# Softmax sums inside the value product, and the division between two 32x32-block turns on VectorE

## The chip, the cores and the metric

One Trainium2 chip, of which the kernel uses one core. The metric is the device time of one execution in microseconds: median of three runs 378.38 (377.3 to 379.06). The profile is of one further execution, whose span from the first to the last instruction is 376.4 us.

## The reference

128 sequences of 64 tokens with 128 features (`x`), and a context of the same shape. Two blocks follow each other.

The first is cross attention with 16 heads of 8 features: queries from the normalised `x`, keys and values from the context.

```
qh, kh, vh = split_heads(q @ W_q + b_q), split_heads(k @ W_k + b_k), split_heads(v @ W_v + b_v)
probs = softmax(einsum('bhqd,bhkd->bhqk', qh, kh) / sqrt(8))
out   = merge_heads(einsum('bhqk,bhkd->bhqd', probs, vh)) @ W_o + b_o
x     = x + tanh(g_xattn) * out
```

The second is a feed-forward network with 8 experts: a small gate picks one expert per token, and the token goes through that expert's two layers (128 to 256 to 128, exact gelu), times its gate probability and tanh(g_ffn), added to `x`.

## The kernel before

All of it is one program with an order written out by hand for each engine. 8192 tokens are 64 tiles of 128 tokens (two sequences of 64); four tiles are a chunk (512 tokens, 16 chunks).

**First stage.** A loop over 76 slots (`SLOTS`, lines 242, 449, 587, 967 and 1242: every engine has the same loop, GpSimd by chunks). In slot k several tiles are under way at once, each with a fixed lag: scores for the row maxima of tile k-4 (`scores1`, L1121), their maxima on VectorE (L976, two halves), final scores of tile k-10 in fp32 (`scores2`, L1104 and L1111), their exponentials on ScalarE in two halves (L596, L598), the value product of tile k-11 and the output projection of tile k-12 (`values`, L1166 to L1198). Once per chunk come the transposes of xn and of the context (L1263, L1216), the projections of keys (L1223), queries (L1281) and values (L1288), and of the maxima (L1271), which ScalarE copies as mS (L645) and GpSimd turns into a mask product MD (L443) that the scores of that chunk need.

The exponentials lie as PT: on the partitions the 64 keys of one head and, below them, the 64 keys of its neighbour; on the columns 16 blocks (8 head pairs of 2 sequences) of 64 queries. For two heads at a time the value product multiplies 32 columns of V (8 of one head that meet only the upper 64 partitions, 8 of the other that meet only the lower 64, 16 zeros) with 64 columns of PT. The result in PSUM (`pv`, columns 0 to 127) holds head and feature on the partitions and tokens on the columns: two such products are added into each group of 32 partitions, the second shifted by 16. The sums of the exponentials come from a second set of matmuls: `kz` holds ones where V holds values, so that `pv` columns 128 to 255 hold each sum eight times, on the partitions where its head's values lie (L1184, eight matmuls of 128 columns). VectorE takes 128x128 reciprocals of them (L982, `rec`), adds the projection of the tile before to the residual (L988, `XR`, with the semaphore x1_ok), and multiplies values and reciprocals (L993, `OT`, ot_ok). TensorE multiplies OT by W_o in the next slot (L1195). In fp32 each matmul is two instructions in the trace.

`values` waits, before its first matmul, for x1_ok and ot_ok of the slot before. Its one signal to VectorE, pv_ps, comes with its last matmul.

In each slot VectorE goes through: maxima (L976), reciprocal, XR, OT, then `stat_sum` (L716) and `stat` (L708) for a later tile's layer norm, and in some slots a part of the routing (peak, lead, pick, count, place, gate: six slots of every twelve, two to four small instructions each). `route_place` waits for GpSimd's g_pay.

GpSimd has in each chunk: the mask product (L443), the layer norm's powers and its four products (L352 to L360, L375), the residual with the bias (L367), the second norm's power (L384, L386), and from chunk 8 on four record sends (L400, an indirect DMA of one tile's rows each into the expert-sorted buffer `records`), later eight.

**Second stage.** 71 tiles of sorted tokens: load (SP), normalise (VectorE), transpose and two layers (TensorE, L1228, L1236, L1323, L1326), gelu (ScalarE), combine (VectorE, L1037), and a scattered store per tile from GpSimd (L471).

Of the kernel before, what the change touches and what calls it, by code (L numbers as in the profile page):

```python
# [13 lines left out]
P = 128  # L14
D = 128
H = 16
# [46 lines left out]
def gated_block(nc, x, ctx_in, g_xattn, g_ffn, W_q, b_q, W_k, b_k, W_v, b_v, W_o, b_o, w_red, wg, W1, b1, W2, b2, out):  # L63
    es = ExitStack()
    with es:
# [6 lines left out]
        def sem(name):  # L72
            return es.enter_context(nc.semaphore(name))
# [20 lines left out]
        kz = sb("kz", [P, 48])  # L94
# [44 lines left out]
        rec = sb("rec", [P, P])  # L139
# [36 lines left out]
        kz_ok, perm_ok, brow_ok, bvb_ok, sel_ok = (sem(n) for n in ("kz_ok", "perm_ok", "brow_ok", "bvb_ok", "sel_ok"))  # L176
# [15 lines left out]
        pv_ps, rec_ok, ot_ok, x1_ok = (sem(n) for n in ("pv_ps", "rec_ok", "ot_ok", "x1_ok"))  # L192
# [485 lines left out]
        def _(dve):  # L678
# [8 lines left out]
            link(nc.vector.memset(kz[:, :], 0.0))  # L687
            nc.vector.memset(kz[0:S, 16:16 + DK], 1.0)
            nc.vector.memset(kz[S:P, 16 + DK:32], 1.0).then_inc(kz_ok, 1)
# [68 lines left out]
            def make_masks():  # L758

                with nc.allow_low_precision("zeros and ones"):  # L760
                    nc.vector.tensor_reduce(imask[:, :], ident[:, :].rearrange("p (a i l) -> p i a l", i=2, l=2),
                                            mybir.AxisListType.XY, ALU.add).then_inc(imask_ok, 1)
                link(nc.vector.tensor_reduce(usum[:, :].rearrange("p (a o) -> p a o", o=1),
                                             ident[:, :].rearrange("p (t a i) -> p a t i", t=RT, i=HI),
                                             mybir.AxisListType.XY, ALU.add))
                dve.wait_ge(par_ok, 1)
                link(nc.vector.tensor_tensor(upar[:, :, :], usum[:, 0:CU].rearrange("p (u o) -> p u o", o=1).to_broadcast([P, CU, 2]),
                                             par[:, :].rearrange("p (o l) -> p o l", o=1).to_broadcast([P, CU, 2]), ALU.mult))
                nc.vector.tensor_copy(usel[:, :, :, :].rearrange("p u l k -> p (u l) k"),
                                      upar[:, :, :].rearrange("p u (l o) -> p (u l) o", o=1).to_broadcast([P, 2 * CU, S])  # L770
                                      ).then_inc(sel_ok, 1)

# [194 lines left out]
            for k in range(SLOTS):  # L967
# [12 lines left out]
                if 0 <= n < NU:  # L980
                    dve.wait_ge(pv_ps, pv_turn(k))
                    nc.vector.reciprocal(rec[:, :], pv[:, P:2 * P]).then_inc(rec_ok, 1)  # L982
# [8 lines left out]
                if 0 <= n < NU:  # L991
                    dve.wait_ge(rec_ok, n + 1)
                    nc.vector.tensor_tensor(OT[n % 2][:, :], pv[:, 0:P], rec[:, :], ALU.mult).then_inc(ot_ok, 1)  # L993
                if j == 1 and 2 <= s < NC + 2:
                    x_logits(s - 2)
                if 2 * CU <= k + 6 < NU:
                    stat_sum(k + 6)
                if 2 * CU <= k + 7 < NU:
                    stat(k + 7)
# [9 lines left out]
                if k == 10:  # L1009
                    split_biases()  # L1010
                if k in gate_done_at:
                    route_gate(gate_done_at[k])
# [48 lines left out]
        def _(pe):  # L1061
# [104 lines left out]
            def values(k):  # L1166
                n, no = k - LAGV, k - LAGO
                if k == LAGV:
                    pe.wait_ge(kz_ok, 1)
                    pe.wait_ge(wox_ok, 1)  # L1170
                if no >= 1:
                    pe.wait_ge(x1_ok, min(no, NU))
                if no >= 0:
                    pe.wait_ge(ot_ok, min(no + 1, NU))
                last = None
                if 0 <= n < NU:
                    c, u = n // CU, n % CU
                    pe.wait_ge(pt_ok, n + 1)
                    if u == 0:
                        pe.wait_ge(v_ok, c + 1)  # L1180
                    vf = V[c % 3][:, :, :, :].rearrange("p u h r -> p (u h r)")
                    for i in range(2):
                        for t in range(RT):
                            nc.tensor.matmul(pv[32 * t:32 * t + 32, P:2 * P].rearrange("p (b q) -> p b q", b=2),  # L1184
                                             kz[:, 16 - 16 * i:48 - 16 * i], PT[n % 2][:, HI * t + i:HI * t + HI:2, :],
                                             start=(i == 0), stop=False, skip_group_check=True)
                    for i in range(2):
                        for b in range(2):
                            for t in range(RT):
                                at = 32 * (H * u + 8 * b + 2 * t + i) - 16 * i  # L1190
                                last = nc.tensor.matmul(pv[32 * t:32 * t + 32, S * b:S * b + S], vf[:, at:at + 32],  # L1191
                                                        PT[n % 2][:, HI * t + 2 * b + i, :], start=False, stop=(i == 1),
                                                        skip_group_check=True)
                if 0 <= no < NU:
                    last = nc.tensor.matmul(pv[:, 2 * P:2 * P + DX], OT[no % 2][:, :], wox[:, :], start=True, stop=True,  # L1195
                                            skip_group_check=True)
# [173 lines left out]
```

## Time and profile before

| | |
|---|---|
| runs, us | 378.38, 377.3, 379.06 |
| span of the profiled execution | 376.4 us (the page gives no other time of it) |
| TensorE busy | 332.6 us (88%) |
| VectorE busy | 290.0 us (77%) |
| GpSimd busy | 266.9 us (71%) |
| ScalarE busy | 242.3 us (64%) |
| mean granted TensorE clock | 0.963 of full speed |

Full speed of TensorE is 2.4 GHz; a granted clock of 0.5 is 1.2 GHz. Busy time is the union of an engine's instructions; consecutive instructions overlap at their ends, so what an instruction costs its engine is read from start to start in a timeline. "Idle before" with a releaser says which engine's semaphore ended a wait; "issue" is time in which the profile shows nothing waited for.

### The profile page before, as it was taken

The numbers are of one execution on the slowest core, as the hardware profiler recorded it, in microseconds if no ns is written. First come the engines' busy times: TensorE is split into PE (matmuls) and PEld (weight loads), VectorE is DVE, ScalarE is ACT, GpSimd is POOL, SyncE is SP. The second block draws the span as 40 slices with busy tenths as digits, with TensorE's granted clock in tenths as the row PEclk, the third lists the DMA queues.
The fourth block names the chain that finished last, engine by engine and source line by source line (L and its number), as shares of the span: only waits on it lengthen the run. The fifth ranks groups of instructions, "written<-read, shape, count | busy, mean of one in ns | idle before, by whom it ended". The sixth has DMA issues, their size and how long they took to land.

```text
span 376.4 us, 17275 instructions
## 1 busy us (share of the span) xinstructions
PE 332.6 (88%) x6654; PEld 261.4 (69%) x6654; DVE 290.0 (77%) x900; ACT 242.3 (64%) x604; POOL 266.9 (71%) x349
## 2 busy tenths in 40 slices
PE   3878999999999999999999997776888999999960
PEld 1534776776776777876876866655776899999950
DVE  7777788889899898989899799966578666666630
ACT  3747688788788788788788885644443455555520
POOL 6494664474685898798796876787557777777771
PEclk9978999999999999999999999997699999999995
DMA  5344334323313423323211121143014433333210
GB/s 114 105 141 141 102 95 129 111 80 98 118 48 98 139 80 105 95 70 102 71 63 51 44 93 50 41 129 97 36 56 132 137 120 99 114 110 100 66 46 0
DMA packets 47164, 34.13 MB, mean 91 GB/s; under 512 B 9800, under 2 KB 42955, under 8 KB 47083
## 3 DMA queue, kind: packets, MB, share of 16 engines
q1 hardware_dynamic: 42440, 23.90, 22.6%
q0 software_dynamic: 4352, 9.00, 6.6%
q8 instruction: 54, 0.88, 1.0%
q14 instruction: 26, 0.21, 0.2%
q10 hardware_dynamic: 292, 0.13, 0.1%
HBM read 17.13 MB, written 10.04 MB: 72 GB/s over the span
## 4 chain that ended last, share of the span: by engine, by line
PE 62%; issue 9%; POOL 9%; DVE 8%; ACT 6%; SPq 2%; DMA 1%; POOLq 0%; DVEq 0%; ACTq 0%
PE m L1326 10%; PE sc L1236 8%; PE pv L1184 7%; POOL records L400 6%; PE pv L1191 5%; PE sc L1111 5%; PE pv L1195 5%; PE m L1288 4%; PE sc L1121 3%; PE sc L1104 3%; PE sc L1228 2%; PE m L1323 2%; ACT PT L598 1%; PE m L1263 1%; PE m L1216 1%
## 5 line engine op out<-in xcount | busy, mean ns | idle before, releaser
L976 DVE TENSOR_REDUCE mx<-sc 128x8 f32<-128x512 f32 x128 | 82.2, 684 | 20.7 <-PE sc L1121 20.2
L471 POOL DMA_INDIRECT out<-fo,rr x71 | 70.0, 986 | 23.3 <-issue 19.3
L400 POOL DMA_INDIRECT records<-XR,pos x64 | 63.4, 991 | 20.4 <-issue 16.4
L982 DVE RECIPROCAL rec<-pv 128x128 f32<-128x128 f32 x64 | 61.1, 954 | 10.4 <-PE pv L1195 5.2
L596 ACT ACTIVATE PT<-sc 128x512 f32<-128x512 f32 x64 | 38.1, 595 | 28.2 <-issue 20.1
L1326 PE MATMUL m<-w,fgT 128*128 x284 | 50.7, 302 | 0.1
L1236 PE MATMUL sc<-fxT,w1s 128*128 128x128 f32 x284 | 45.6, 284 | 4.2 <-DVE w1s L964 3.3
L1037 DVE SCALAR_TENSOR_TENSOR fo<-m,rr 128x128 f32<-128x128 f32 x71 | 24.9, 350 | 29.8 <-PE m L1326 29.8
L1184 PE MATMUL pv<-PT,kz 128*32 128x128 f32 x1024 | 41.7, 281 | 6.5 <-DVE XR L988 5.9
L375 POOL TENSOR_SCALAR xn<-XC,mv,rstd 128x128 f32<-128x128 f32 x56 | 44.2, 799 | 0.0
L1236 PEld LDWEIGHTS sc<-fxT,w1s 128*128 128x128 f32 x284 | 38.6, 197 | 6.5 <-ACT fxT L578 4.2
L578 ACT ACTIVATE fxT<-sc 128x128 f32<-128x128 f32 x71 | 19.7, 278 | 35.4 <-PE sc L1228 35.4
L1191 PE MATMUL pv<-PT,V 128*32 128x64 f32 x2048 | 41.3, 220 | 0.2 <-issue 0.2
L1326 PEld LDWEIGHTS m<-w,fgT 128*128 128x128 f32 x284 | 38.0, 194 | 2.6 <-issue 0.4
L1111 PE MATMUL sc<-Qd,kT 32*128 32x128 f32 x1024 | 39.8, 270 | 0.0
L584 ACT ACTIVATE fgT<-sc 128x256 f32<-128x256 f32 x71 | 27.3, 384 | 18.7 <-PE sc L1236 18.3
L598 ACT ACTIVATE PT<-sc 128x512 f32<-128x512 f32 x64 | 38.3, 598 | 0.0
L1191 PEld LDWEIGHTS pv<-PT,V 128*32 128x32 f32 x2048 | 37.6, 111 | 0.3 <-issue 0.3
L1184 PEld LDWEIGHTS pv<-PT,kz 128*32 128x32 f32 x1024 | 24.5, 109 | 14.5 <-DVE XR L988 7.2
L1111 PEld LDWEIGHTS sc<-Qd,kT 32*128 32x128 f32 x1024 | 34.4, 186 | 0.0
L1195 PE MATMUL pv<-wox,OT 128*128 128x137 f32 x128 | 32.5, 336 | 0.0
L352 POOL TENSOR_TENSOR rstd<-ve,mhalf 128x4 f32<-128x4 f32 x16 | 16.5, 1034 | 21.6 <-DVE ve L721 21.4
(207 smaller groups left out, 681.3 us busy)
## 6 DMA issues: line engine op xcount, KB each, us to landing
rr<-records SPq DMA_DIRECT2D x71, 72.0 KB, 2.0
XC<-in_x SPq DMA_DIRECT2D x16, 256.0 KB, 3.2
C<-in_ctx SPq DMA_DIRECT2D x16, 256.0 KB, 3.1
Qd<-Qf SPq DMA_DIRECT2D x64, 64.0 KB
Kd<-kb SPq DMA_DIRECT2D x64, 32.0 KB
w<-in_L_ffn_W SPq DMA_DIRECT2D x16, 128.0 KB, 2.8
out<-fo,rr POOLq DMA_INDIRECT x71, 2.3
w1l<-in_L_ffn_W SPq DMA_DIRECT2D x8, 128.0 KB, 3.3
```

The source lines that it names most:

```text
L375: i = nc.gpsimd.tensor_scalar(xn[:, u, :], XC[c % 3][:, u, :], mv[c % 2][:, u, 0:1], rstd[:, u:u + 1], ALU.subtract, ALU.mult)
L400: nc.gpsimd.indirect_dma_start(out=records, out_offset=bass.IndirectOffsetOnAxis(ap=pos[:, u:u + 1], axis=0), in_=XR[:, u, :], in_offset=N ...
L471: nc.gpsimd.indirect_dma_start(out=out_rows, out_offset=bass.IndirectOffsetOnAxis(ap=rr[q][:, R_ID:R_ID + 1].bitcast(U32), axis=0), in_=fo ...
L598: nc.scalar.activation(pt[:, 2:4], sc[:, 2:4, 256:512], ACT.Exp).then_inc(pt_ok, 1)
L976: nc.vector.tensor_reduce(mx[c % 2][:, t:t + 2, HI * u:HI * u + HI], sc[:, t:t + 2, 0:256].rearrange("p t (i k) -> p t i k", i=HI), AX_X, ...
L982: nc.vector.reciprocal(rec[:, :], pv[:, P:2 * P]).then_inc(rec_ok, 1)
L1111: m = nc.tensor.matmul(sc[:, t, 256 + P * b:256 + P * b + P].rearrange("p (i q) -> p i q", i=2), kT[c % 3][r, u, b, :, :].rearrange("r l k ...
L1184: nc.tensor.matmul(pv[32 * t:32 * t + 32, P:2 * P].rearrange("p (b q) -> p b q", b=2), kz[:, 16 - 16 * i:48 - 16 * i], PT[n % 2][:, HI * t ...
L1191: last = nc.tensor.matmul(pv[32 * t:32 * t + 32, S * b:S * b + S], vf[:, at:at + 32], PT[n % 2][:, HI * t + 2 * b + i, :], start=False, st ...
L1195: last = nc.tensor.matmul(pv[:, 2 * P:2 * P + DX], OT[no % 2][:, :], wox[:, :], start=True, stop=True, skip_group_check=True)
L1236: i = nc.tensor.matmul(sc[:, 2 + p, P * m:P * m + P], w1s[p][:, P * m:P * m + P], fxT[p][:, :], start=True, stop=True, skip_group_check=True)
L1326: i = nc.tensor.matmul(o, fgT[p][:, m, :], w2[:, bass.ds(e, 1), m, :].rearrange("p o c -> p (o c)"), start=False, stop=(m == HH - 1), skip ...
```

## The change

V gets its sums: two more of the 32 columns that each pair of heads has hold a one on the upper, and on the lower 64 partitions (columns 16 and 17), written once per buffer by `v_sums` from `hsel`. ScalarE rewrites only columns 0 to 15 for each chunk. So each value product also yields the two heads' sums. The products of even and odd pairs are no longer added into one another but go to columns of their own, and fill 256 columns of `pv`.

VectorE turns these 256 columns in blocks of 32x32 into `TV`, which puts tokens on the partitions; there a head's sum is one number per token, and 16 reciprocals per partition do for 128. `NV` is the product of values and reciprocals with the 14 idle columns left out, and a second turn of 128 columns brings OT back into its old form. XR, stat_sum and stat are set between the four steps.

TensorE's value product waits for the first turn (`tv_ok`) and x1_ok; the wait for ot_ok moves to in front of the projection.

```diff
-            link(nc.vector.memset(kz[:, :], 0.0))
-            nc.vector.memset(kz[0:S, 16:16 + DK], 1.0)
-            nc.vector.memset(kz[S:P, 16 + DK:32], 1.0).then_inc(kz_ok, 1)
+            link(nc.vector.memset(hsel[:, :], 0.0))
+            nc.vector.memset(hsel[0:S, 0:1], 1.0)
+            nc.vector.memset(hsel[S:P, 1:2], 1.0).then_inc(hsel_ok, 1)
...
+            def v_sums(i):
+
+                dve.wait_ge(hsel_ok, 1)
+                dve.wait_ge(zero_p, i + 1)
+                nc.vector.tensor_copy(V[i][:, :, :, 2 * DK:2 * DK + 2].rearrange("p u h r -> p (u h) r"),
+                                      hsel[:, :].rearrange("p (o l) -> p o l", o=1).to_broadcast([P, CU * H, 2])
+                                      ).then_inc(vden_ok, 1)
...
-                    nc.vector.reciprocal(rec[:, :], pv[:, P:2 * P]).then_inc(rec_ok, 1)
+                    nc.vector.transpose(TV[:, :, :].rearrange("p a r -> p (a r)"), pv[:, 0:2 * P]).then_inc(tv_ok, 1)
...
+                    dve.wait_ge(tv_ok, n + 1)
+                    nc.vector.reciprocal(rec[:, :, :], TV[:, :, 2 * DK:2 * DK + 2]).then_inc(rec_ok, 1)
+                if 2 * CU <= k + 6 < NU:
+                    stat_sum(k + 6)
+                if 0 <= n < NU:
                     dve.wait_ge(rec_ok, n + 1)
-                    nc.vector.tensor_tensor(OT[n % 2][:, :], pv[:, 0:P], rec[:, :], ALU.mult).then_inc(ot_ok, 1)
+                    nc.vector.tensor_tensor(NV[:, :, :, :], TV[:, :, 0:2 * DK].rearrange("p a (l d) -> p a l d", l=2),
+                                            rec[:, :, :].rearrange("p a (l o) -> p a l o", o=1).to_broadcast([P, 2 * CU, 2, DK]),
+                                            ALU.mult).then_inc(nv_ok, 1)
+                if 2 * CU <= k + 7 < NU:
+                    stat(k + 7)
+                if 0 <= n < NU:
+                    dve.wait_ge(nv_ok, n + 1)
+                    nc.vector.transpose(OT[n % 2][:, :], NV[:, :, :, :].rearrange("p a l d -> p (a l d)")).then_inc(ot_ok, 1)
                 if j == 1 and 2 <= s < NC + 2:
                     x_logits(s - 2)
-                if 2 * CU <= k + 6 < NU:
-                    stat_sum(k + 6)
-                if 2 * CU <= k + 7 < NU:
-                    stat(k + 7)
...
+                if k in (3, 4, 7):
+                    v_sums((3, 4, 7).index(k))
...
                 if k == LAGV:
-                    pe.wait_ge(kz_ok, 1)
+                    pe.wait_ge(vden_ok, 3)
                     pe.wait_ge(wox_ok, 1)
                 if no >= 1:
                     pe.wait_ge(x1_ok, min(no, NU))
-                if no >= 0:
-                    pe.wait_ge(ot_ok, min(no + 1, NU))
...
+                    if n >= 1:
+                        pe.wait_ge(tv_ok, n)
                     vf = V[c % 3][:, :, :, :].rearrange("p u h r -> p (u h r)")
-                    for i in range(2):
-                        for t in range(RT):
-                            nc.tensor.matmul(pv[32 * t:32 * t + 32, P:2 * P].rearrange("p (b q) -> p b q", b=2),
-                                             kz[:, 16 - 16 * i:48 - 16 * i], PT[n % 2][:, HI * t + i:HI * t + HI:2, :],
-                                             start=(i == 0), stop=False, skip_group_check=True)
                     for i in range(2):
                         for b in range(2):
                             for t in range(RT):
-                                at = 32 * (H * u + 8 * b + 2 * t + i) - 16 * i
-                                last = nc.tensor.matmul(pv[32 * t:32 * t + 32, S * b:S * b + S], vf[:, at:at + 32],
-                                                        PT[n % 2][:, HI * t + 2 * b + i, :], start=False, stop=(i == 1),
-                                                        skip_group_check=True)
+                                at = 32 * (H * u + 8 * b + 2 * t + i)
+                                last = nc.tensor.matmul(
+                                    pv[32 * t:32 * t + 32, P * b:P * b + P].rearrange("p (h i q) -> p i h q", h=2, i=2)[:, i],
+                                    vf[:, at:at + 32], PT[n % 2][:, HI * t + 2 * b + i, :].rearrange("p (h q) -> p h q", h=2),
+                                    start=True, stop=True, skip_group_check=True)
                 if 0 <= no < NU:
+                    pe.wait_ge(ot_ok, no + 1)
                     last = nc.tensor.matmul(pv[:, 2 * P:2 * P + DX], OT[no % 2][:, :], wox[:, :], start=True, stop=True,
                                             skip_group_check=True)
```

## Rows read from the trace of the kernel before

**Rows 1.** Table of stretches: length, busy us (instructions) by engine, PEclk, DMA, GB/s.

```profile
core 0: us, PE busy (x) PEld busy (x) DVE busy (x) ACT busy (x) POOL busy (x), PEclk, DMA share, GB/s
38.90:118.90 80.00, 77.99 (x2074) 58.97 (x2071) 68.55 (x184) 64.64 (x149) 46.86 (x88) 1.00 0.35 101
118.90:214.76 95.86, 94.19 (x2516) 71.27 (x2508) 84.57 (x229) 79.42 (x187) 81.72 (x105) 1.00 0.26 82
214.76:256.80 42.04, 33.73 (x1028) 26.48 (x1020) 36.09 (x121) 25.21 (x67) 31.33 (x36) 1.00 0.27 81
256.80:269.30 12.50, 9.03 (x84) 7.64 (x78) 7.60 (x27) 5.18 (x18) 8.06 (x9) 0.61 0.17 54
```

**Rows 2.** Timeline of TensorE in one slot: start, length, line, count.

```profile
171.24 0.29 PE L1104 MATMUL sc<-MD,usel 32*128 32x256 bf16 x4
...
171.91 0.32 PE L1121 MATMUL sc<-Kd,qb 32*64 32x256 bf16 x8
172.16 0.64 PE L1184 MATMUL pv<-PT,kz 128*32 128x128 f32 x16
172.62 0.63 PE L1191 MATMUL pv<-PT,V 128*32 128x64 f32 x32
173.18 0.50 PE L1195 MATMUL pv<-wox,OT 128*128 128x137 f32 x2
...
174.57 0.29 PE L1104 MATMUL sc<-MD,usel 32*128 32x256 bf16 x4
```

**Rows 3.** Timeline of ScalarE: exponentials of one slot and of the next.

```profile
159.35 0.60 ACT L596 ACTIVATE PT<-sc 128x512 f32<-128x512 f32 x1 [1.02 <-issue]
...
159.90 0.60 ACT L598 ACTIVATE PT<-sc 128x512 f32<-128x512 f32 x1
...
162.75 0.60 ACT L596 ACTIVATE PT<-sc 128x512 f32<-128x512 f32 x1
```

**Rows 4.** Groups of instructions by line (whole run, reciprocal of 12 of 120:214).

```profile
L976 DVE TENSOR_REDUCE mx<-sc 128x8 f32<-128x512 f32 x128 | 82.2, 684 | 20.7 <-PE sc L1121 20.2
...
L982 DVE RECIPROCAL rec<-pv 128x128 f32<-128x128 f32 x64 | 61.1, 954 | 10.4 <-PE pv L1195 5.2
...
L993 DVE TENSOR_TENSOR OT<-pv,rec 128x128 f32<-128x128 f32 x64 | 17.9, 280 | 0.0
...
L862 DVE RECIPROCAL col<-col 128x12 f32<-128x12 f32 x2 | 0.5, 228 | 0.1
```

**Rows 5.** Timeline of VectorE in one slot.

```profile
184.29 0.96 DVE L982 RECIPROCAL rec<-pv 128x128 f32<-128x128 f32 x1
185.16 0.26 DVE L988 SCALAR_TENSOR_TENSOR XR<-pv,tg,XR 128x137 f32<-128x137 f32 x1
185.34 0.28 DVE L993 TENSOR_TENSOR OT<-pv,rec 128x128 f32<-128x128 f32 x1
...
186.33 1.29 DVE L976 TENSOR_REDUCE mx<-sc 128x8 f32<-128x512 f32 x2 [0.44 <-PE sc L1121]
```

**Rows 6.** GpSimd: waits (total, times, longest) of 126:257, and its timeline.

```profile
POOL MD L443 <- ACT mS L645: 8.5, 7, 2.1
POOL records L400 <- DVE XR L863: 1.6, 2, 0.8
...
186.07 0.60 POOL L443 TENSOR_TENSOR MD<-mS,imask 128x256 bf16<-128x256 bf16 x1 [1.23 <-ACT mS L645]
...
200.28 0.60 POOL L443 TENSOR_TENSOR MD<-mS,imask 128x256 bf16<-128x256 bf16 x1 [1.27 <-ACT mS L645]
```

**Rows 7.** Timeline: products on VectorE with both inputs in SBUF, and GpSimd beside them.

```profile
149.93 3.15 POOL L375 TENSOR_SCALAR xn<-XC,mv,rstd 128x128 f32<-128x128 f32 x4
...
150.63 0.24 DVE L845 TENSOR_TENSOR ky<-ky,oh 128x96 f32<-128x96 f32 x1
...
228.85 0.61 POOL L443 TENSOR_TENSOR MD<-mS,imask 128x256 bf16<-128x256 bf16 x1 [2.10 <-ACT mS L645]
...
229.13 0.41 DVE L817 TENSOR_TENSOR ex<-ex,col 128x64 f32<-128x64 f32 x1
```

**Rows 8.** GpSimd's stores, by line, 269.3 to 368.7 us.

```profile
L471 POOL DMA_INDIRECT out<-fo,rr x71 | 70.0, 986 | 23.3 <-issue 19.3 <-DVE fo L1037 4.0
```

More of the change, by code:

```diff
@@ L93, in gated_block @@
         clog = sb("clog", [P, NX])
-        kz = sb("kz", [P, 48])
+        hsel = sb("hsel", [P, 2])
         usum = sb("usum", [P, 8])
@@ L138, in gated_block @@
         PT = [sb(f"PT{i}", [P, H, S]) for i in range(2)]
-        rec = sb("rec", [P, P])
+        TV = sb("TV", [P, 2 * CU, 32])
+        rec = sb("rec", [P, 2 * CU, 2])
+        NV = sb("NV", [P, 2 * CU, 2, DK])
         OT = [sb(f"OT{i}", [P, P]) for i in range(2)]
@@ L175, in gated_block @@
         pstep, one_ok = sem("pstep"), sem("one_ok")
-        kz_ok, perm_ok, brow_ok, bvb_ok, sel_ok = (sem(n) for n in ("kz_ok", "perm_ok", "brow_ok", "bvb_ok", "sel_ok"))
+        hsel_ok, vden_ok, perm_ok, brow_ok, bvb_ok, sel_ok = (sem(n) for n in ("hsel_ok", "vden_ok", "perm_ok", "brow_ok", "bvb_ok", "sel_ok"))
         bcol_ps, b16_ok, tg_ok, bvo_ps, tgbo_ok = (sem(n) for n in ("bcol_ps", "b16_ok", "tg_ok", "bvo_ps", "tgbo_ok"))
@@ L191, in gated_block @@
         s1_ps, mxa_ok, mx_ok, mT_ps, mS_ok, s2_ps, pt_ok = (sem(n) for n in ("s1_ps", "mxa_ok", "mx_ok", "mT_ps", "mS_ok", "s2_ps", "pt_ok"))
-        pv_ps, rec_ok, ot_ok, x1_ok = (sem(n) for n in ("pv_ps", "rec_ok", "ot_ok", "x1_ok"))
+        pv_ps, tv_ok, rec_ok, nv_ok, ot_ok, x1_ok = (
+            sem(n) for n in ("pv_ps", "tv_ok", "rec_ok", "nv_ok", "ot_ok", "x1_ok"))
         gsq_ok, gve_ok, g_pay, xw_ps, xwT_ok, xwt_ps, lgx_ok = (
```

## The prediction

> **What bounds the kernel now.** I read the table of stretches first [rows 1]. From 38.9 to 118.9 us and on to 214.8 us TensorE is busy 97 to 98% of the time at the full clock (2.4 GHz). From 214.8 to 256.8 it is 80%, with VectorE at 86%. For the second stage, after 269.3 us, I read GpSimd's line of stores: 71 scattered stores of 0.986 us, 19.3 us of issue in front of them (some 0.3 each), and only 4.0 us of true waiting for VectorE in all [rows 8]. So attention is bound by TensorE, and the second stage by GpSimd's stores, 70.0 + 19.3 of its 99 us.
>
> Next the timeline of TensorE in one slot (one tile of 128 tokens) [rows 2]: weights and scores start at 171.24, the sums against kz at 172.16, the values at 172.62, the output projection at 173.18, and the next slot's scores at 174.57. Starts are what count, since the ends overlap: kz takes 0.46 us, the values 0.56.
>
> GpSimd decides what a faster TensorE can be worth. Its mask product L443 runs once per chunk (4 slots): from 186.07 to 200.28 is 14.21 us, and the row at 200.28 says that 1.27 of them were a wait for ScalarE's mS [rows 6]. So GpSimd has 12.94 us of its own work in a chunk that sends four records. From the first record (126.2 us) to 256.8 us it waited 8.5 us for mS in 7 waits, and twice for gates, 1.6 us of which 0.3 is issue [rows 6]: 9.8 us in 130. That is a floor under the change.
>
> **The change part by part.** Removed from TensorE: the 16 passes of L1184, 0.46 us of every slot. The 32 passes of the values stay: as many weight loads, as many columns; only where they write changes, so I leave them at 0.56. Their start no longer waits for OT; they wait for x1 and for the first turn, which stand earlier on VectorE than OT did. The projection alone waits for OT.
>
> How much of 0.46 comes out? The scores of a slot wait for the exponentials of the one before, and those for the row maxima: scores done 0.99 us after the slot begins (0.67 to L1121, 0.32 its length [rows 2]), first reduction 0.68 [rows 4], two exponentials 0.55 (159.35 to 159.90) and 0.60 [rows 3], and some 0.17 for four handovers: 3.0 us. No slot can be shorter. Of the four slots of a chunk, the two with the projections of keys and queries are at 3.3 us (171.24 to 174.57 [rows 2]); 14.2 less twice 3.3 leaves 3.8 for each of the other two, which can give 0.45 each, while the first two can give 0.3 each at most, say 0.27. Against it stands ScalarE in the slot with kb and kT: from one exponential (159.35) to the next (162.75) it took 3.40 us and never waited; against 3.0 that takes 0.40 back [rows 3]. Sum: 0.90 + 0.54 - 0.40 = 1.0 us per chunk, 14.1 to 13.1. Ends for this term: 0.5 (only the two heavy slots, with something lost) and 1.84 (the full 4 x 0.46).
>
> VectorE, starts again [rows 5]: the reciprocal of 128 holds it 0.87 us (184.29 to 185.16), and XR, 0.26 us long, 0.18: the next may start some 0.08 before the end. By that OT takes 0.20 of its 0.28, the two statistics 0.09 and 0.18, and all ends at 185.89, where the 0.44 of idle time before the next maxima begins. Taken out: 0.87 + 0.20 = 1.07. Put in: a turn of 256 columns out of PSUM, 16 reciprocals, a product of 128, a turn of 128. The trace has no turn on VectorE. Between the reduction of 512 (684 ns) and the product of 128 (280 ns) [rows 4] the slope is 1.05 ns per element; I take it for both turns, as the nearest rows: 0.42 and 0.28 us long, 0.33 and 0.20 as steps. The other end is the reciprocal's rate: (954 - 228) / (128 - 12) = 6.3 ns per element [rows 4]. 16 reciprocals: 0.25. A step that needs the one before cannot start until that has ended, but XR, stat_sum and stat stand between the four, and fill the time. In order: turn 0, XR 0.33, reciprocals 0.51, stat_sum 0.66, product 0.79, stat 0.99, turn 1.17, end 1.37, against 1.52 now (0.87 + 0.18 + 0.20 + 0.27). VectorE gains 0.15 per slot, close to nothing, though 0.87 is removed. It has 0.40 us idle in a slot now; in a 3.27 us slot it has some 0.3. The routing work, 0.4 to 0.8 us in six of each twelve slots, will at times come late; that I have in the 1.0.
>
> The Trainium skill, "VectorE: DVE Perf Modes", section "The three transpose paths", gives 311 ns for a 128x128 turn in bf16; with it for the second turn the slot would be 0.03 longer, which moves nothing. No row here shows a turn.
>
> The rule that speaks against the change is one of ports. What the rows show: a product with both inputs in SBUF that started inside GpSimd's L443 (228.85, 0.61 us long) took 0.41 us at 229.13 for 64 elements, and ended 0.08 after L443; but the same kind of product at 150.63 took 0.24 for 96 elements while GpSimd ran xn (149.93, four of them in 3.15 us) [rows 7]. The new product NV has both inputs in SBUF where the old OT read PSUM. The Trainium skill, "SBUF — State Buffer", section "Who interferes with whom", says that such an instruction contends with any GpSimd instruction that reads SBUF, and that the second to issue is fully blocked. By that rule xn would have held the product at 150.63, and the trace does not agree there; at L443 it does. I take it for L443 alone: 0.2 us in one slot of four at worst, under 0.1 us per chunk. It is a rival below.
>
> Set-up: three copies of 128 elements (0.25 us each) at slots 3, 4, 7, where VectorE waits for TensorE: nothing. SP's and GpSimd's queues get no new instruction.
>
> **The sum**, against the span. From the first values (38.9) to 118.9: 80 us / 14.2 = 5.6 chunks x 1.0 = 5.6. From there to 256.8 GpSimd's floor decides: of its 9.8 us of waits I leave 1.5 (chunks of 13.1 against its 12.9, seven times): 8.3 (ends 4 and 9.8). At the hand-over to the second stage (256.8 to 269.3, clock 0.61 on average, that is mostly 1.2 GHz [rows 1]) three rounds of TensorE - VectorE - TensorE lose the reciprocal in front of XR (0.87 to 0.33 each), and kz in the one slot at half clock, but GpSimd's seven records (1.26 us each, as the stores are [rows 8]) and a gate (1.3, an estimate from its two small instructions) end at about 267, which allows 2.3: I take 1.6. In the second stage nothing changes: it is GpSimd's 71 stores. Together 15.5: span 376.4 to 360.9. The page gives no other time of its execution; the runs have a median of 378.38, 2.0 above the span, so 362.9: **363 us**. Its own range is 359 to 367.
>
> **Rivals.** (A) VectorE sets the pace. If a turned element costs twice what I took (2.1 ns), the slot grows by 0.40 - 0.15 = 0.25 and VectorE, with its routing, needs about 13.6 per chunk. Then 5.6 x 0.5 = 2.8, GpSimd's waits shrink by only 4.5, hand-over 1: 8.3, 370 us. For it: VectorE is already busy 88% of 118.9 to 214.8 [rows 1], and reductions wait for TensorE only 0.44. Against: one read and one write per element are all that a turn needs, as in the reduction. (B) The port rule holds fully: NV meets a reading GpSimd instruction (about 8 of 13 us) and waits 0.25 on average, and GpSimd in turn is held some 0.8 per chunk. 4.5 + 4 + 1.5 = 10, 368.5 us. Against it the row at 150.63. (C) Slower: a turn of 4-byte data runs on VectorE like a reciprocal, several cycles per element. Place: VectorE between pv_ps and ot_ok in every slot. Price at 6.3 ns: (256 + 128) x 5.25 = 2.0 us per slot, less 0.15 and the idle 0.40: 1.5 x 64 = 94 us, 472 us; at 4.2 ns (the slope times four) 0.67 x 64 = 43, 421 us. It decides from about 2.5 ns per element on: below, VectorE's idle time and the reciprocal hide it. Nothing in the trace speaks for it but that no turn is in it. (D) More than forecast: kz's removal lets the hand-over stay at 2.4 GHz (the fall came after TensorE stood still 2 us behind XR; the new wait is 0.5 to 0.8 shorter) and GpSimd's waits go entirely: 5.6 x 1.2 + 9.8 + 2.3 = 19, 359 us or a little less. The opposite of that is possible too: TensorE, with less work from 240 us on, falls to 1.2 GHz sooner, which costs up to 4 us; it is in the range's upper side. That the change does not do what it says is hardly possible: L1184 and L982 are gone by the diff.
>
> **Chances.** Forecast 0.61, A 0.14, B 0.06, C 0.10, D 0.09. What this kernel's measurement can tell from no change is about 0.5%, 1.9 us. C is slower; a weaker A (2.4 ns) ends within 0.5%: faster 0.85, same 0.04, slower 0.11. The range leaves out C and the far ends: 357 to 371.
>
> **What would show it.** Values start 0.25 us after L1121 in a full slot; chunks of about 13.1 us up to 118 us of old time, and L443's waits under 0.3 us each from there on; the turn of 256 at 0.42 us and of 128 at 0.28; VectorE's steps from the first turn to the end of the last 1.4 us; NV at 0.28 except beside L443; the second stage as long as before (99 us). Wrong would be: turns over 0.6 us; reductions that no longer wait for TensorE at all while L443 does wait; a longer second stage.

## The result and the profile after

The kernel after takes **364.72 us** (median of 4 runs, 361.58 to 366.57), the kernel before 378.53 beside it: ratio **0.964**, 95% interval 0.959 to 0.970. The profiled execution of after has a span of 364.8 us and a time of 366.57, so it is the slowest of its four; the other three have spans of 359.9 to 364.0. Below, a median is over all executions of a kernel, and a ratio and its interval leave out the few that ran slower than their fellows at a lower granted clock.

The page of after, its groups of instructions: line, engine, names, shapes, count | busy us, mean ns | idle before and its releaser. They answer to [rows 4] and, with the stores (L474), to [rows 8].

```profile
L987 DVE TENSOR_REDUCE mx<-sc 128x8 f32<-128x512 f32 x128 | 82.3, 684 | 18.0 <-PE sc L1142 17.7
L474 POOL DMA_INDIRECT out<-fo,rr x71 | 70.0, 986 | 23.1 <-issue 19.3 <-DVE fo L1058 3.8
...
L993 DVE STREAM_TRANSPOSE TV<-pv 128x256 f32<-128x256 f32 x64 | 28.2, 441 | 1.3 <-PE pv L1213 1.3
...
L1009 DVE TENSOR_TENSOR NV<-TV,rec 128x128 f32<-128x128 f32 x64 | 19.2, 301 | 0.6
L1016 DVE STREAM_TRANSPOSE OT<-NV 128x128 f32<-128x128 f32 x64 | 19.1, 298 | 0.6
...
L1004 DVE RECIPROCAL rec<-TV 128x16 f32<-128x16 f32 x64 | 15.3, 239 | 0.0
```

The steps of VectorE in a slot, as its timeline in after has them (the statistics between them left out); they answer to [rows 5].

```profile
59.91 1.29 DVE L987 TENSOR_REDUCE mx<-sc 128x8 f32<-128x512 f32 x2 [0.25 <-PE sc L1142]
61.12 0.44 DVE L993 STREAM_TRANSPOSE TV<-pv 128x256 f32<-128x256 f32 x1
61.48 0.32 DVE L999 SCALAR_TENSOR_TENSOR XR<-pv,tg,XR 128x137 f32<-128x137 f32 x1
61.72 0.24 DVE L1004 RECIPROCAL rec<-TV 128x16 f32<-128x16 f32 x1
...
62.12 0.28 DVE L1009 TENSOR_TENSOR NV<-TV,rec 128x128 f32<-128x128 f32 x1
...
62.52 0.29 DVE L1016 STREAM_TRANSPOSE OT<-NV 128x128 f32<-128x128 f32 x1
...
63.15 1.29 DVE L987 TENSOR_REDUCE mx<-sc 128x8 f32<-128x512 f32 x2 [0.26 <-PE sc L1142]
...
64.36 0.44 DVE L993 STREAM_TRANSPOSE TV<-pv 128x256 f32<-128x256 f32 x1
...
65.65 0.29 DVE L1016 STREAM_TRANSPOSE OT<-NV 128x128 f32<-128x128 f32 x1
```

VectorE has as much to do as before. In a plain slot it needs 1.58 us from the first turn to the end of the last, statistics included (64.36 to 65.94), for 1.60 before (184.29 to 185.89). The slot shown is the one of four with an extra step of the layer norm, and takes 1.69. The next maxima still wait for TensorE, but 0.26 us in place of the 0.44 of [rows 5]; and the idle time in front of VectorE's first step behind the values, 10.4 us in all before [rows 4], is 1.3.

The table of stretches of after, cut at the same events as [rows 1] (the tenth rstd on GpSimd; the mask product at 214.76 in before; the end of GpSimd's last gate product; the first store; and then the second stage).

```profile
core 0: us, PE busy (x) PEld busy (x) DVE busy (x) ACT busy (x) POOL busy (x), PEclk, DMA share, GB/s
38.90:114.54 75.64, 70.37 (x1767) 50.41 (x1771) 68.89 (x237) 66.28 (x155) 49.88 (x91) 1.00 0.38 108
114.54:204.71 90.17, 85.78 (x2140) 60.98 (x2136) 83.72 (x289) 79.89 (x190) 82.31 (x104) 1.00 0.27 86
204.71:246.62 41.91, 31.32 (x780) 22.82 (x778) 36.27 (x144) 24.57 (x66) 31.49 (x36) 0.88 0.27 82
246.62:257.54 10.92, 7.58 (x59) 6.28 (x60) 7.54 (x31) 4.83 (x16) 8.06 (x11) 0.61 0.20 63
257.54:356.90 99.36, 90.32 (x693) 80.96 (x692) 63.70 (x240) 45.12 (x137) 73.64 (x75) 0.98 0.32 94
```

The gain, stretch by stretch: 4.3 us up to the first mark (118.88 to 114.54), 5.7 in the second (95.86 to 90.17), 0.1 in the third, where the granted clock is now 0.88 in place of 1.00, and 1.6 in the hand-over (12.50 to 10.92). The second stage is as long as it was. Sum 11.7; the spans differ by 11.6.

One slot on TensorE's timeline in after, to be held against [rows 2].

```profile
166.53 0.29 PE L1125 MATMUL sc<-MD,usel 32*128 32x256 bf16 x4 [0.51 <-POOL MD L446]
...
167.20 0.32 PE L1142 MATMUL sc<-Kd,qb 32*64 32x256 bf16 x8
167.44 0.65 PE L1207 MATMUL pv<-PT,V 128*32 128x64 f32 x32
168.03 0.50 PE L1213 MATMUL pv<-wox,OT 128*128 128x137 f32 x2
168.37 1.02 PE L1299 MATMUL m<-xT,wqp 128*128 128x512 f32 x2
169.56 0.29 PE L1125 MATMUL sc<-MD,usel 32*128 32x256 bf16 x4 [0.17 <-ACT PT L601]
```

The values start 0.24 us after L1142 and the projection 0.59 after them: 0.46 us per slot has gone, and the values cost 0.03 more than before (0.59 for 0.56). TensorE now stands still at the head of a slot, here for GpSimd's mask and in the next slot for the exponentials.

GpSimd in after: its waits of 114.5 to 246.6 (total us, times, longest) and its timeline. They answer to [rows 6].

```profile
POOL MD L446 <- ACT mS L648: 3.0, 2, 2.6
```

```profile
126.90 0.62 POOL L446 TENSOR_TENSOR MD<-mS,imask 128x256 bf16<-128x256 bf16 x1
...
204.71 0.62 POOL L446 TENSOR_TENSOR MD<-mS,imask 128x256 bf16<-128x256 bf16 x1
217.12 0.68 POOL L446 TENSOR_TENSOR MD<-mS,imask 128x256 bf16<-128x256 bf16 x1 [0.35 <-ACT mS L648]
231.95 0.61 POOL L446 TENSOR_TENSOR MD<-mS,imask 128x256 bf16<-128x256 bf16 x1 [2.62 <-ACT mS L648]
```

From 126.90 to 204.71, six chunks of 12.97 us, no mask product waits: that is GpSimd's own work, and the floor was there. Where a chunk sent no records, before 100 us, the masks are 12.74 us apart.

### The profile page after: what moved, and what is told of

Read it like the earlier page. It is cut to its first block, busy times and chain, and to the rows that moved or that the text cites. A ratio compares the mean times of both kernels' runs of the same rounds, so it can differ in the third digit from the quotient of the medians.

```text
span 364.8 us, 15361 instructions
## 1 busy us (share of the span) xinstructions
PE 314.0 (86%) x5630; PEld 237.8 (65%) x5630; DVE 286.6 (79%) x1031; ACT 240.4 (66%) x604; POOL 268.1 (73%) x349
## 4 chain that ended last, share of the span: by engine, by line
PE 44%; POOL 17%; DVE 16%; issue 8%; ACT 8%; SPq 2%; DMA 1%; POOLq 0%; DVEq 0%; ACTq 0%
PE m L1344 10%; PE sc L1254 9%; POOL records L403 6%; POOL xn L378 4%; PE sc L1132 4%; DVE mx L987 3%; PE m L1306 3%; PE pv L1207 3%; PE pv L1213 2%; ACT PT L601 2%; PE sc L1142 2%; PE sc L1125 2%; PE sc L1246 2%; PE m L1341 2%; ACT PT L599 2%
## 5 line engine op out<-in xcount | busy, mean ns | idle before, releaser
L474 POOL DMA_INDIRECT out<-fo,rr x71 | 70.0, 986 | 23.1 <-issue 19.3
L1207 PE MATMUL pv<-PT,V 128*32 128x64 f32 x2048 | 43.6, 227 | 5.4 <-DVE XR L999 4.8
L1207 PEld LDWEIGHTS pv<-PT,V 128*32 128x32 f32 x2048 | 32.8, 112 | 13.7 <-DVE XR L999 5.5
L1132 PE MATMUL sc<-Qd,kT 32*128 32x128 f32 x1024 | 41.3, 278 | 0.0
L1132 PEld LDWEIGHTS sc<-Qd,kT 32*128 32x128 f32 x1024 | 35.9, 193 | 0.0
L1213 PE MATMUL pv<-wox,OT 128*128 128x137 f32 x128 | 33.5, 345 | 0.5 <-DVE OT L1016 0.4
L1125 PEld LDWEIGHTS sc<-MD,usel 32*128 32x128 bf16 x256 | 6.8, 91 | 41.3 <-ACT PT L601 22.3
L1125 PE MATMUL sc<-MD,usel 32*128 32x256 bf16 x256 | 18.9, 284 | 15.5 <-ACT PT L601 13.1
L993 DVE STREAM_TRANSPOSE TV<-pv 128x256 f32<-128x256 f32 x64 | 28.2, 441 | 1.3 <-PE pv L1213 1.3
```

Source lines behind the costliest of these rows:

```text
L474: nc.gpsimd.indirect_dma_start(out=out_rows, out_offset=bass.IndirectOffsetOnAxis(ap=rr[q][:, R_ID:R_ID + 1].bitcast(U32), axis=0), in_=fo ...
L1125: nc.tensor.matmul(sc[:, t, 256:512].rearrange("p (b i q) -> p i b q", b=2, i=2), usel[r, u, :, :].rearrange("r l k -> r (l k)"), MD[c % 2 ...
L1132: m = nc.tensor.matmul(sc[:, t, 256 + P * b:256 + P * b + P].rearrange("p (i q) -> p i q", i=2), kT[c % 3][r, u, b, :, :].rearrange("r l k ...
L1207: last = nc.tensor.matmul(pv[32 * t:32 * t + 32, P * b:P * b + P].rearrange("p (h i q) -> p i h q", h=2, i=2)[:, i], vf[:, at:at + 32], PT ...
```

## The experiments

The kernels ran on several chips. On two of them (kz_kept, kz_once, rec_small and turn_twice on one; kz_once_again, after_again, xn_dve and xn_dve_late on the other) the kernel before takes 465 us and the changed one 440, where it is 377 to 379 and 365 elsewhere. The chunks of after_again and after match up to about 110 us (12.73 and 12.74 us each from 57 to 85 us). Later after_again has idle times that no wait of the kernel explains, even between the matmuls of one group: 5.3 us in front of matmuls of the values from 120 to 210 us, where after has none. So from these two chips only ratios on the same chip and rows before 110 us carry an argument.

**kz_kept: the sums' matmuls put back beside the change.** Eight matmuls of ones per slot, into columns that nothing reads, ahead of the values:

```diff
+for i in range(2):
+    for t in range(RT):
+        nc.tensor.matmul(pv[32*t:32*t+32, 400:512]..., kz[:, 16-16*i:48-16*i], PT[n % 2][:, HI*t+i:HI*t+HI:2, 0:56], ...)
```

> The changed kernel with TensorE's old load put back: in every slot eight matmuls of ones against 112 of PT's columns, into PSUM columns that nothing reads (the old ones had 128 columns, some 0.40 against 0.46 us of a slot). VectorE does the new work. My theory, that the gain comes from TensorE's part: 375 to 378 us, chunks of about 13.9 us. Rival, that VectorE's lighter division brings it: no more than 1 or 2 us above the changed kernel (about 366).

Measured: 466.40 us, before 465.10, ratio 1.003 (0.999 to 1.006). The whole gain is gone.

**kz_once: TensorE's part of the change alone.** The kernel before; the sums run for tile 0 only, and VectorE keeps its 128 reciprocals:

```diff
-for i in range(2):
+for i in range(2 if n == 0 else 0):
     for t in range(RT):
         nc.tensor.matmul(pv[32 * t:32 * t + 32, P:2 * P]..., kz[:, 16 - 16 * i:48 - 16 * i], ...
```

> The kernel before with only TensorE's part of the change: the sums are made for the first tile alone and left standing, so later tiles are divided by the first tile's sums; the 128 reciprocals and the old product stay on VectorE. Theory: most of the gain is there, 365 to 369 us, a few us above the changed kernel because XR, behind 0.87 us of reciprocals, comes later and VectorE's slot is 0.15 us longer. Rival (VectorE must get lighter too before TensorE's 0.46 us can come out): 374 or more.

Measured: 439.85 us, ratio 0.943 (0.936 to 0.950). It was run again with the changed kernel beside it, as kz_once_again and after_again.

> The kernel before with the eight matmuls of the sums left out for every tile but the first (the division takes the first tile's sums); VectorE's part stays as it was, with 128 reciprocals. On another chip this took more off than the whole change (0.943 against 0.964). My theory: TensorE's eight matmuls are the gain, and VectorE's sequence after them (one reciprocal of 954 ns and a product, against two turns, a reciprocal and a product) is the same length within 0.2 us, so the ratio lies within 0.006 of the changed kernel's: 0.960 to 0.972, 363 to 367 us. Rival, the two turns cost more than they save: this kernel is faster than the changed one by more than 2 us, below 0.958. Rival, the small reciprocal carries part of the gain: slower than the changed one by more than 2 us, above 0.972.

> The changed kernel again, unaltered, as the partner on this chip of the three kernels beside it. Every theory: ratio to the kernel before 0.962 to 0.967, near 364 us; masks (MD) 13.0 us apart between 127 and 204 us without a wait for mS.

Measured: kz_once_again 442.37 (0.952, 0.947 to 0.957), after_again 439.65 (0.948, 0.943 to 0.954). On this chip the change brings more than the 0.964 that I expected, but the two kernels differ by 0.3% only, within their intervals: TensorE's part is the change's whole gain, and VectorE's part is worth nothing that these intervals, about 0.5% to each side, can tell. kz_once was not run on a chip where before takes 377 us; there the two pool kernels below have to do.

**rec_small: a shorter VectorE on the kernel before.** 16 reciprocals and one product that spreads them, with no turn, 0.7 us per slot less on VectorE:

```diff
-nc.vector.reciprocal(rec[:, :], pv[:, P:2 * P])
+nc.vector.reciprocal(rec[:, 0:16], pv[:, P:P + 16])
```

> The kernel before with only VectorE made lighter: 16 reciprocals in place of 128 and one product with them spread out, so each group of eight columns is divided by the sum of another query; TensorE's matmuls all stay. VectorE loses 0.7 us per slot, far more than the change takes from it. Theory (TensorE bound): 375 to 378 us, the little that is gained coming after the chunks' loads end, where TensorE waits for XR. Rival (VectorE's reciprocals were the bound): 366 or less.

Measured: 460.23, ratio 0.988 (0.983 to 0.993). A quarter of what the change brings on such a chip (0.948, below), for five times the 0.15 that I had VectorE gain; and none of it before 110 us, as the masks below say.

**turn_twice: the first turn doubled.** The changed kernel with the turn of 256 columns done once more into a buffer that nothing reads:

```diff
+nc.vector.transpose(TV2[:, :, :].rearrange("p a r -> p (a r)"), pv[:, 0:2 * P])
 nc.vector.transpose(TV[:, :, :].rearrange("p a r -> p (a r)"), pv[:, 0:2 * P]).then_inc(tv_ok, 1)
```

> The changed kernel with a second turn of the same 256 columns before the real one, into a tile that nothing reads: 0.36 us more of VectorE in each slot, as if a turned element cost twice. By the prediction's rival A: VectorE sets the pace, chunks of about 13.6 to 13.9 us, 370 to 373 us. If VectorE had room left in a slot (0.26 us idle before the maxima), under 368.

Measured: 444.79, ratio 0.958 (0.951 to 0.966). Most of the gain stays with 0.4 us more on VectorE in every slot.

The masks of two successive chunks on GpSimd's timeline tell kz_kept, kz_once, rec_small and turn_twice apart without the chip's later idle times. In this order:

```profile
75.12 0.61 POOL L447 TENSOR_TENSOR MD<-mS,imask 128x256 bf16<-128x256 bf16 x1 [3.80 <-ACT mS L649]
88.99 0.61 POOL L447 TENSOR_TENSOR MD<-mS,imask 128x256 bf16<-128x256 bf16 x1 [3.85 <-ACT mS L649]
```

```profile
72.26 0.61 POOL L443 TENSOR_TENSOR MD<-mS,imask 128x256 bf16<-128x256 bf16 x1 [2.70 <-ACT mS L645]
84.99 0.61 POOL L443 TENSOR_TENSOR MD<-mS,imask 128x256 bf16<-128x256 bf16 x1 [2.73 <-ACT mS L645]
```

```profile
73.98 0.61 POOL L443 TENSOR_TENSOR MD<-mS,imask 128x256 bf16<-128x256 bf16 x1 [4.04 <-ACT mS L645]
88.02 0.61 POOL L443 TENSOR_TENSOR MD<-mS,imask 128x256 bf16<-128x256 bf16 x1 [4.08 <-ACT mS L645]
```

```profile
69.12 0.61 POOL L447 TENSOR_TENSOR MD<-mS,imask 128x256 bf16<-128x256 bf16 x1 [2.91 <-ACT mS L649]
81.86 0.61 POOL L447 TENSOR_TENSOR MD<-mS,imask 128x256 bf16<-128x256 bf16 x1 [2.90 <-ACT mS L649]
```

A chunk is 13.87 us with the matmuls (kz_kept) and 14.04 in rec_small, as in before (14.03); it is 12.73 in the kernel without them (kz_once), though VectorE is as before, and 12.74 in turn_twice, as in after. So up to here the pace is TensorE's and the scores - maxima - exponentials loop's. VectorE's groups of turn_twice over 50 to 100 us say how near it was:

```profile
L988 DVE TENSOR_REDUCE mx<-sc 128x8 f32<-128x512 f32 x32 | 20.5, 684 | 0.7 <-PE sc L1144 0.7
L994 DVE STREAM_TRANSPOSE TV<-pv 128x256 f32<-128x256 f32 x15 | 6.6, 440 | 0.0
L995 DVE STREAM_TRANSPOSE TV<-pv 128x256 f32<-128x256 f32 x15 | 6.1, 406 | 0.0
```

0.7 us of waiting in fifteen slots: the slack is used up. Once the routing work comes on top, the next chunks are 13.6 us (81.86 to 95.48) and 16.0 us, against 12.9 in after_again. The 16.0 are not the turn's alone. Two products of VectorE in that chunk lie beside a product of GpSimd and end some 0.15 us after it: L861 takes 1.42 us (102.63) beside one of 1.29, and NV 1.33 us (106.38) beside one of 2.36.

**pool_before and pool_after: 0.9 us more for GpSimd per chunk.** A fill of 1024 columns that nothing reads, in chunks 9 to 14, put into both kernels:

```diff
     gate_norm(s - 4)
+if 9 <= s < 15:
+    nc.gpsimd.memset(pad[:, :], 0.0)
```

> The kernel before with 0.9 us more of GpSimd's own time (a fill of a tile that nothing reads, writing only) in each of the six chunks that hold both four record sends and a layer norm. It waited 0.5 to 1.3 us for ScalarE in each of them. Theory: most of it is hidden, 378.5 to 381 us. Pair with the next run.

> The changed kernel with the same 0.9 us of GpSimd in the same six chunks. Theory (GpSimd is the floor there, it never waits from 127 to 217 us): all 5.4 us come through, about 370 us, so that the gap between before and after shrinks by 3 to 5 us against the change's own. Rival (TensorE still sets the pace there): 365 to 367.

Measured on one chip (before 376.93): pool_before 377.65, ratio 1.003 (0.999 to 1.007). pool_after has a median of 370.63, but its four executions lie from 365.61 to 372.74, too far apart to say whether all of the 5.4 us came through. The trace decides. GpSimd's timeline of pool_after:

```profile
140.77 0.62 POOL L447 TENSOR_TENSOR MD<-mS,imask 128x256 bf16<-128x256 bf16 x1
...
196.21 0.62 POOL L447 TENSOR_TENSOR MD<-mS,imask 128x256 bf16<-128x256 bf16 x1
```

Four chunks in 55.44 us, 13.86 each, against 13.03 in after (139.73 to 191.86): 0.83 of the 0.9 comes through (the fill is 0.95 us long). In pool_before the same four chunks take 55.34 us apart (144.87 to 200.21), where before has 56.23 (144.05 to 200.28): hidden, and even 0.2 us per chunk shorter, for which I have no cause. So GpSimd's work is the floor after the change and was not one before.

**kz_late: filler columns where the clock fell.** The changed kernel with kz_kept's matmuls for tiles 50 to 63 alone (`range(2 if n >= 50 else 0)`).

> The changed kernel with matmuls of ones (8 of 112 columns, into PSUM that nothing reads) added only from tile 50 on, where TensorE now idles up to 40% and its clock was 1.2 GHz for 12 us (221 to 233 us). If the lost activity brought the clock down and the clock cost time there: clock 1.0 until the hand-over and 362 us or less in the median. If the extra matmuls cost as much as the clock gives back: no difference, 364 to 366. If the fall has other causes: it stays, and 366 to 368.

Measured: 362.89, ratio 0.962 (0.956 to 0.968). The stretch of 221 to 233 us, first in after, then in before, then in kz_late:

```profile
221.00:233.00 12.00, 11.37 (x240) 8.31 (x232) 10.50 (x39) 5.72 (x17) 7.69 (x10) 0.57 0.13 42
```

```profile
221.00:233.00 12.00, 9.61 (x305) 7.74 (x297) 11.62 (x40) 7.71 (x21) 8.09 (x10) 1.00 0.20 66
```

```profile
221.00:233.00 12.00, 8.52 (x255) 6.53 (x254) 11.17 (x43) 7.27 (x21) 8.65 (x11) 1.00 0.15 46
```

In after TensorE ran here mostly at 1.2 GHz (0.50 from 224 us on), after slots in which it had stood still 1.4 to 1.6 us for the exponentials (216.93 and 220.74); in kz_late, with the columns of ones, it kept 2.4 GHz up to the hand-over. The mean clock of whole executions agrees: 0.966 to 0.975 in five of kz_late's six, 0.935 to 0.957 in after's four. What that is worth is less plain, as two kernels without the columns say (pool_after and ot_front, below). Times in us:

| | mask of the 14th to that of the 16th chunk | from there to the first store | granted clock 0.50 before 248 us in |
|---|---|---|---|
| before | 27.39 | 27.17 | none |
| after | 27.24 | 25.59 | 224 to 232 |
| kz_late | 26.20 | 25.47 | none |
| pool_after | 25.60 | 25.49 | 228 to 232, 244 to 248 |
| ot_front | 25.48 | 28.81 | 238 to 248 |

ot_front stood still just as long (1.44 and 1.56 us, at 219.11 and 222.91) and kept the full clock to 234 us. So where the clock falls differs between executions, and the 1.0 us between after and kz_late in the first column is no more than the kernels without the columns of ones differ by among themselves. The two ratios are not apart.

**ot_front: the wait for OT put back ahead of the values.** The changed kernel with `pe.wait_ge(ot_ok, ...)` moved from the projection to the front of `values`.

> The changed kernel with the wait for OT back in front of the values, the rest unchanged: undoes the moved wait. Theory: OT is ready 0.9 us before the values in the slots with maxima, so nothing there; in the last eight slots TensorE would start its values 0.7 us later each, most of it under GpSimd's sends: 0 to 2 us longer than the changed kernel, 364 to 367.

Measured: 368.07, ratio 0.976 (0.969 to 0.983), above the changed kernel's 0.964 (0.959 to 0.970), with intervals that just meet. The trace puts little of this down to the wait. One slot shows it at work (95.50 to 99.85 us, 4.35 long where its fellows take 3.03): TensorE starts its values only when OT has been turned. GpSimd, VectorE and TensorE there:

```profile
94.73 2.35 POOL L395 TENSOR_TENSOR w<-w,w1l 128x1024 f32<-128x1024 f32 x1
...
95.05 2.18 DVE L1009 TENSOR_TENSOR NV<-TV,rec 128x128 f32<-128x128 f32 x1
...
97.35 0.29 DVE L1016 STREAM_TRANSPOSE OT<-NV 128x128 f32<-128x128 f32 x1
97.74 0.65 PE L1209 MATMUL pv<-PT,V 128*32 128x64 f32 x32 [1.26 <-issue]
```

That is 1.3 us. Three more losses are no waits for OT. The slot before is 4.92 us long because 1.26 us pass between the 21st and the 22nd of the 32 passes of its values (after has a smaller such gap there: that group takes 1.02 us for 0.65, at 91.70). The chunks from 58.70 to 85.08 us take 13.19 us for 12.74, with values that start on time, 0.25 us after L1142, and last up to 0.89. And behind 232 us stand the 3.2 us of the table above, where the clock is 0.50; in those last slots the moved wait may have a share. What it is worth as a whole stays open.

**xn_dve and xn_dve_late: GpSimd's floor lowered.** Chunks 9 to 15: the fourth of the normalised tiles on VectorE, in slot 2 of the chunk before, under a semaphore of its own; and the same with kz_late's columns.

```diff
-for u in range(CU):
+for u in range(CU - (c >= 9)):
     i = nc.gpsimd.tensor_scalar(xn[:, u, :], XC[c % 3][:, u, :], ...)
...
+if j == 2 and 9 <= s + 1 < NC:
+    dve.wait_ge(rstd_ok, s + 2); dve.wait_ge(xT_ps, s + 1)
+    nc.vector.tensor_scalar(xn[:, 3, :], XC[(s + 1) % 3][:, 3, :], ...).then_inc(xnv_ok, 1)
```

> The changed kernel with the last of the four normalised tiles (xn) of chunks 9 to 15 computed on VectorE in the third slot of a chunk, in place of GpSimd. Theory that GpSimd's own 13.0 us of work per chunk is the floor from 127 to 204 us: it loses 0.78 us of work per chunk there, the slots' own pace of 12.75 us (measured earlier in the kernel) plus VectorE's added tile of about 0.2 us in one slot takes over at 12.7 to 12.9, GpSimd waits for mS again, and the time falls by 0.7 to 2 us: 362 to 364. Rival, GpSimd sits at a floor that TensorE or VectorE shares, so that nothing is gained: within 0.5 us of the changed kernel. Rival, VectorE's wait for rstd or the added tile lengthens the slots: 1 to 3 us slower.

> The kernel with the moved tile, and with the eight matmuls of ones added for tiles 50 to 63 alone, which kept TensorE at the full granted clock from 215 to 247 us in an earlier run and gained 1 to 2 us. If the two gains add: 1 to 2 us below the kernel with the moved tile alone, 360 to 363 us, the fastest of all. If the fall of the clock comes from elsewhere or the added columns cost what the clock gives: the same within 0.5 us.

Measured: xn_dve 446.57 (0.954, 0.948 to 0.960) and xn_dve_late 452.61 (0.974, 0.968 to 0.980), beside after_again at 439.65 (0.948, 0.943 to 0.954). The first is not shown to be slower, since the intervals overlap; the second is, and it is also slower than the first: on this chip the columns of ones cost 2%, where they cost nothing that shows in kz_late. GpSimd's timeline of xn_dve_late, before its columns of ones begin:

```profile
146.00 0.60 POOL L452 TENSOR_TENSOR MD<-mS,imask 128x256 bf16<-128x256 bf16 x1 [3.92 <-ACT mS L654]
162.27 0.60 POOL L452 TENSOR_TENSOR MD<-mS,imask 128x256 bf16<-128x256 bf16 x1 [4.25 <-ACT mS L654]
```

On that chip a chunk takes 16 us here and GpSimd waits 4 of them (2.2 to 3.7 in after_again), so its floor isn't the bound and couldn't be tested. What these two would do at 365 us stays open, and no version that beats the changed kernel was found.

## Why the prediction was right, step by step

**363 us forecast, 364.72 measured**, as faster, for the reason given; but of the 15.5 us of the sum the profiled execution shows 11.6, and the median lies 1.9 us below that execution: terms A and B were off, in the same direction, and that the spread of the runs hid half of it was luck.

- **What bounds it.** Right. TensorE: on the chips where before takes 465 us, removing its eight matmuls alone gives the whole gain (kz_once), and putting them back takes it all (kz_kept). GpSimd's floor of 12.94 us: 12.97 measured, and pool_before and pool_after show it from both sides. Second stage: 99.4 and 99.36 us.
- **The slot, 1.0 us per chunk.** Under-sized: 14.04 to 12.74, 1.30. By slots, from the starts of TensorE's first scores (L1104, L1125): 3.23, 3.54, 3.81, 3.46 became 3.24, 3.10, 3.37, 3.03. The floor of 3.0 holds. The two slots without projections of keys and queries (3.81 and 3.46, not 3.8 each as I had read) gave 0.44 and 0.43, close to the 0.45 that I said. Of the other two the one with the queries gave 0.44 and not 0.27, and the one with the keys, where ScalarE makes kb and kT, gave nothing, where I had charged 0.40 against a 0.27: together 0.43 and not 0.14.
- **Term A, 5.6 us to the first mark.** 4.3. By the slots it should have been 6.6; the start-up took 2.3 back (the second mask product at 47.30 us against 45.00). I gave start-up no spread. The changed kernel had that mask at 43.16 in after_again, and kernels equal to it up to there at 43.70 (kz_late), 44.96 (ot_front) and 47.13 (pool_after); so this belongs to the execution and not to the change. The table of stretches has TensorE at 1.2 GHz through 24 to 36 us in after, and at 0.65 to 1.00 there in before; here one window of each, after first:

```profile
24.00:28.00 4.00, 3.17 (x24) 1.22 (x20) 3.30 (x9) 3.77 (x12) 4.00 (x8) 0.50 0.36 107
```

```profile
24.00:28.00 4.00, 2.54 (x47) 1.72 (x48) 3.18 (x9) 2.35 (x10) 3.89 (x5) 0.92 0.25 78
```

- **Term B, 8.3 us.** The step that failed. 5.7 came up to 204.71, where GpSimd's waits for mS went from 5.1 us to none (the mask at 204.71 included); beyond it 2.6 were due and 0.1 came. There the waits were 3.0 in 2 for 3.4 before. The chunk from 204.71 took 12.41 us (14.09 in before), the next 14.83 (13.30), while TensorE fell to 1.2 GHz. I had named that fall, but only as the range's upper side (up to 4 us). At the full clock that chunk is 13.51 (kz_late) and 13.08 (ot_front), with 4 us at the half clock 13.57 (pool_after). So the fall is part of the answer, some 1.0 to 1.8 us over the two chunks by the table at kz_late, as far as single executions can say; the cause of the rest stays open. In the terms of the sum: I let GpSimd's floor decide up to 256.8 us and left 1.5 us of waits, but 3.0 were left, all behind 204.71, where ScalarE's mS still came after GpSimd was free.
- **Term C, 1.6 us.** 12.50 to 10.92: 1.6, with the clock at 0.61 in both.
- **VectorE's sequence, 1.37 us.** Too short: 1.58 in plain slots (1.69 in the fourth, 61.12 to 62.81), so VectorE gained 0.02 and not 0.15. The turns are 0.44 and 0.29 us (0.42 and 0.28 said), the reciprocals 0.24; but XR right behind the turn takes 0.32 and not 0.26, NV to OT is 0.42 as a step where I had 0.38, and I had counted the last turn by its step, 0.20, where its end was asked. It cost nothing in the plain slots, which turn_twice shows can bear 0.4 more until the routing comes.
- **OT's wait at the projection.** I counted the moved wait as nothing by itself. ot_front's trace shows it worth 1.3 us in the one slot where VectorE is very late, and nothing in the plain ones; the rest of ot_front's 1% is not shown to be its.
- **Ports.** Between rule and row, as I put it: during xn NV takes 0.29 to 0.31 us in ten cases of eleven, and once 0.42; beside L446 0.66. But in after_again it takes 0.38 to 0.71 during xn in seven cases of twelve, so xn is not harmless either. Timeline of after, GpSimd and VectorE:

```profile
158.75 3.12 POOL L378 TENSOR_SCALAR xn<-XC,mv,rstd 128x128 f32<-128x128 f32 x4
...
159.70 0.42 DVE L1009 TENSOR_TENSOR NV<-TV,rec 128x128 f32<-128x128 f32 x1
...
232.05 0.66 DVE L1009 TENSOR_TENSOR NV<-TV,rec 128x128 f32<-128x128 f32 x1
```

  What I missed is the long product of `fold_bias`: NV took 2.18 us beside it in ot_front, and ended 0.15 after it did. The Trainium skill, "SBUF — State Buffer", section "Who interferes with whom", has a VectorE instruction with two SBUF inputs contend with a GpSimd instruction that reads SBUF, for a port pair that only one of them holds at a time. The traces agree for GpSimd's products of two inputs, which NV outlasts by 0.15 us each time (2.18 us beside L395, 0.66 beside L446), and for xn only in part.
- **Rivals.** A (VectorE paces): not here, but turn_twice comes close to that case: 0.958 against after_again's 0.948 on another chip, 1% with intervals that overlap, where the rival had 2% (370 for 363). B: no, by NV's 301 ns on average. C (a turn like a reciprocal): no, 1.7 ns per element for 256 columns, all in. D: no; its opposite came, in part.

## What to carry to other kernels

Find the engine that is second before pricing what you take from the first: here 0.46 us per slot on TensorE was worth 0.33 where nothing else was near, and 0.27 where GpSimd's own 12.97 us per chunk took over. A wait is cheap where its producer is punctual and dear in the few slots where it is not (1.3 us in one slot of ot_front), so put it at the first instruction that needs the data, even if the average slot shows no gain. An engine that has been made to stand still may be granted the lower clock: the saved time can come back as a slow stretch, which the table of stretches shows and the totals hide. And where that stretch falls differed from execution to execution, so one trace of each kernel does not price it.

## What the runs showed of the hardware

- A turn by 32x32 blocks of 4-byte data on VectorE: 441 ns for 256 columns out of PSUM, 298 ns for 128 from SBUF to SBUF, close to a product of the same size (301 ns).
- A reciprocal is the dear one: 954 ns for 128 elements per partition, 239 for 16.
- XR, with the same shapes, takes 320 ns behind the turn and 263 in before; rec_small has 293. Why was not tried.
- A product of two SBUF inputs on VectorE can stand still for all of a like product on GpSimd: 2.18 us in place of 0.29 (ot_front), 1.33 and 1.42 us (turn_twice).
- The same program can run at the full TensorE clock in one execution and at half of it in another: from 28 to 36 us after has 0.50 and after_again 1.00.
